# A graph layer with a linear transformer on one core: three PSUM banks for the edge sums, two for VectorE's shared ring

## The reference, cut to what matters

```
xn = layernorm(x)
# 1. graph attention over 100,000 edges, 4 heads of 64
feats = xn @ Ws + bs
score = a_s[src] + a_d[dst] + aw_e * edge_weight + ab
w     = exp(-relu(score / 20))
gnn   = segment_sum(w * feats[dst], src) / segment_sum(w, src)
# 2. four layers of a linear transformer (8 heads of 32, feed-forward of 1024)
for i in range(4):
    h = layernorm(x) * g + b
    q, k = softmax(h @ Wq, over features), softmax(h @ Wk, over nodes)
    x = x + (q @ (k.T @ (h @ Wv))) @ Wo + bo
    x = x + gelu(layernorm(x) * g + b @ W1 + b1) @ W2 + b2
x = x_in + gnn + mix
# 3. slice attention: softmax of 512 slice logits per node, tokens, weighted sums
x = x + slice_attention(layernorm(x))
```

## Time and profile before

| | us |
|---|---|
| median of three runs | 3382.09 (3379.09 to 3383.73) |
| span of the profiled execution | 3482.0 |
| TensorE busy in it | 3221.5 |
| VectorE busy | 2347.5 |
| GpSimd busy | 2056.9 |
| ScalarE busy | 1184.5 |

### The profile page before, as it was taken

The page is one execution under the profiler, slowest core; times in us unless marked ns, Lnnn a source line. Parts: engine busy times, 40 slices in busy tenths (PEclk is TensorE's granted clock), DMA queues, the critical chain, the costliest instruction groups (busy, mean ns, idle before and its releaser), DMA issues.

```text
span 3482.0 us, 43961 instructions
## 1 busy us (share of the span) xinstructions
PE 3221.5 (93%) x13869; PEld 2325.5 (67%) x13869; DVE 2347.5 (67%) x6155; ACT 1184.5 (34%) x2126; POOL 2056.9 (59%) x1776
## 2 busy tenths in 40 slices
PE   8888999999899999999889899898999998999989
PEld 6665667777677777767566666576666666665668
DVE  7998888854454555545677777676666666769951
ACT  3443333333233333323333334243342424422320
POOL 3330577777777777777377677773777777711100
PEclk9999999999999999999999999899999999999999
DMA  3422122222322222322355454454455555422125
GB/s 115 144 96 78 37 50 44 49 49 43 81 47 47 49 50 44 76 55 58 101 136 141 130 138 136 125 141 138 134 152 143 147 147 146 132 82 71 69 101 174
DMA packets 226182, 339.26 MB, mean 97 GB/s; under 512 B 51501, under 2 KB 179755, under 8 KB 225702
## 3 DMA queue, kind: packets, MB, share of 16 engines
q0 software_dynamic: 67840, 119.33, 16.2%
q1 hardware_dynamic: 119502, 162.08, 14.4%
q10 hardware_dynamic: 38616, 55.04, 5.0%
HBM read 248.16 MB, written 87.29 MB: 96 GB/s over the span
## 4 chain that ended last, share of the span: by engine, by line
PE 63%; DVE 21%; issue 5%; another core or an unknown queue 5%; POOL 2%; ACT 2%; DMA 1%; DVEq 1%; ACTq 0%; SPq 0%
PE bank_v L1817 16%; PE bank_a L1804 16%; PE bank_e L1859 8%; PE bank_v L1749 4%; PE bank_a L1721 3%; PE bank_v L1792 3%; PE bank_a L1643 3%; PE bank_v L1709 3%; PE bank_v L1967 2%; POOL arena L804 2%; DVE acc L1503 1%; DVE st L1080 1%; DVEq L1511 1%; DVE arena L1243 1%
## 5 line engine op out<-in xcount | busy, mean ns | idle before, releaser
L804 POOL DMA_INDIRECT arena<-gather_table,arena x880 | 954.7, 1085 | 456.2 <-issue 247.4
L846 POOL DMA_INDIRECT edge_records<-acc x800 | 969.3, 1212 | 402.9 <-issue 402.9
L1817 PE MATMUL bank_v<-W_sb,gT 128*125 128x256 f32 x3200 | 747.1, 385 | 18.3 <-issue 13.7
L1804 PE MATMUL bank_a<-hT,W_sb 128*128 128x500 f32 (+1 forms) x1664 | 716.1, 578 | 13.8 <-issue 12.3
L1817 PEld LDWEIGHTS bank_v<-W_sb,gT 128*125 128x125 f32 x3200 | 602.7, 191 | 122.0 <-issue 26.1
L1804 PEld LDWEIGHTS bank_a<-hT,W_sb 128*128 128x128 f32 x1664 | 317.4, 194 | 326.2 <-issue 307.2
L1859 PE MATMUL bank_e<-arena 128*125 128x260 f32 x1760 | 467.9, 410 | 5.6 <-issue 3.1
L881 ACT ACTIVATE gT<-bank_a,cols 128x500 f32<-128x500 f32 (+1 forms) x416 | 274.2, 661 | 466.1 <-PE bank_a L1804 375.1
L1859 PEld LDWEIGHTS bank_e<-arena 128*125 128x125 f32 x1760 | 327.5, 197 | 57.8 <-issue 7.7
L881 ACT ACTIVATE hT<-bank_a,cols 128x500 f32<-128x500 f32 (+1 forms) x208 | 145.6, 747 | 491.5 <-PE bank_a L1643 378.2
L1239 DVE TENSOR_TENSOR arena<-arena 128x1024 f32<-128x1024 f32 x220 | 268.3, 1220 | 0.0
(11 more groups left out here) (292 smaller groups left out, 4366.1 us busy)
## 6 DMA issues: line engine op xcount, KB each, us to landing
residual<-xs SPq DMA_DIRECT2D x60, 500.0 KB
xs<-residual SPq DMA_DIRECT2D x58, 500.0 KB
arena<-edge_rows ACTq DMA_DIRECT2D x220, 125.0 KB
queries<-qT_out SPq DMA_DIRECT2D x48, 500.0 KB
qT_in<-queries ACTq DMA_DIRECT2D x39, 500.0 KB
arena<-gather_table,arena POOLq DMA_INDIRECT x880
edge_records<-acc POOLq DMA_INDIRECT x800
slice_weights<-arena SPq DMA_DIRECT2D x12, 1000.0 KB, 5.0
```

Of the source, the lines that this page charges most:

```text
L804: e.indirect_dma_start(g_of(j)[:, i, :], None, table_d, bass.IndirectOffsetOnAxis(ap=node[:, TE * j + i:TE * j + i + 1].bitcast(I32), axis ...
L846: e.indirect_dma_start(rec_d, bass.IndirectOffsetOnAxis(ap=pos_i[:, f:f + 1], axis=0), r3[:, f, :], None).then_inc(d_rec, 16)
L1804: o = e.matmul(b[:, 0:n], W[:, k, f * P:(f + 1) * P], hv[:, k, 0:n], start=k == 0, stop=k == KC - 1)
L1817: o = e.matmul(b[0:R, i % 2 * D:(i % 2 + 1) * D], gv[:, f, i * R:(i + 1) * R], W2_sb[:, f * D:(f + 1) * D], start=f == 0, stop=f == FB - 1)
```

## The change

`bank_v` goes from three banks to two and `bank_e` from two to three. The two sums of a block no longer have a bank each: slots 2k and 2k+1 of a rotation over three banks hold the halves of `edge k`, and the score products lie in the bank of slot 2k. TensorE sums the second half of a block in `edge_half k` instead of `edge k`; VectorE adds it there too, and GpSimd's `gather(k+1)` is issued there. The waits follow: TensorE's `edge k` waits for VectorE's second add of `edge_half k-2` instead of the first add of `edge k-1`, and `edge_half k` waits for the first add of `edge k-1`. The list gets two more `edge_half` items.

```diff
-        if k <= NB + 2:
-            blocks.append(((k + 0.5) * apart, ("edge_half", k)))
+        blocks.append(((k + 0.5) * apart, ("edge_half", k)))
...
-        bank_v = [... for i in range(3)]
-        bank_e = [... for i in range(2)]
-        ps_sum = [b[0:R, 0:ROW] for b in bank_e]
-        ps_as = bank_e[0][:, 272:272 + TE * 3 * HG]
+        bank_v = [... for i in range(2)]
+        bank_e = [... for i in range(3)]
+        ps_sum = lambda k, h: bank_e[(2 * k + h) % NE3][0:R, 0:ROW]
+        ps_as = lambda k: bank_e[2 * k % NE3][:, 272:272 + TE * 3 * HG]
...  GpSimd
-                    elif 5 <= k < NB - 1:
-                        e.wait_ge(e_full[1], k - 4)
-                        gather(k + 1)
+                elif stage == "edge_half" and 5 <= at[0] < NB - 1:
+                    k, = at
+                    e.wait_ge(e_full[1], k - 4)
+                    gather(k + 1)
...  VectorE, edge
-                        for h in range(2):
-                            to = accv[:, bass.ds(row_at[h], ROW)]
-                            if h:
-                                e.wait_ge(e_done[0], k - 1)
-                                e.wait_ge(e_full[1], k - 4)
-                            e.tensor_tensor(to, to, ps_sum[h], ALU.add).then_inc(e_done[h], 1)
-                    elif k >= 2:
+                        to = accv[:, bass.ds(row_at[0], ROW)]
+                        e.tensor_tensor(to, to, ps_sum(k, 0), ALU.add).then_inc(e_done[0], 1)
+                    if k >= 2:
                         e.wait_ge(e_done[0], k - 1)
...  VectorE, edge_half, ahead of one_hot_T and one_hot
+                    if k >= 5:
+                        e.wait_ge(e_full[1], k - 4)
+                        to = accv[:, bass.ds(row_at[1], ROW)]
+                        e.tensor_tensor(to, to, ps_sum(k, 1), ALU.add).then_inc(e_done[1], 1)
...  TensorE, edge
-                    if k > 2:
-                        e.wait_ge(e_done[0], k - 2)
+                    if k >= 7:
+                        e.wait_ge(e_done[1], k - 6)
+                    elif k >= 5:
+                        e.wait_ge(e_done[0], k - 4)
...
-                        for h in range(2):
-                            if h and j:
-                                e.wait_ge(e_done[1], j)
-                            for i in range(TH * h, TH * (h + 1)):
+                        for i in range(TH):
...
+                elif stage == "edge_half" and at[0] >= 5:
+                    k, = at
+                    j = k - 5
+                    e.wait_ge(e_done[0], k - 2)
+                    for i in range(TH, TE):
+                        o = e.matmul(ps_sum(k, 1), oh_ring[j % NO][:, i * R:(i + 1) * R], g_of(j)[:, i, :],
+                                     start=i == TH, stop=i == TE - 1)
+                    o.then_inc(e_full[1], 1)
```

More of the change, by code:

```diff
@@ L370, in build_program @@
         bank_a = [ctx.enter_context(nc.psum_tensor(f"bank_a{i}", [P, 512], F32)) for i in range(3)]
-        bank_v = [ctx.enter_context(nc.psum_tensor(f"bank_v{i}", [P, 512], F32)) for i in range(3)]
-        bank_e = [ctx.enter_context(nc.psum_tensor(f"bank_e{i}", [P, 512], F32)) for i in range(2)]
-        ps_sum = [b[0:R, 0:ROW] for b in bank_e]
-        ps_as = bank_e[0][:, 272:272 + TE * 3 * HG]
-        NA, NV = len(bank_a), len(bank_v)
+        bank_v = [ctx.enter_context(nc.psum_tensor(f"bank_v{i}", [P, 512], F32)) for i in range(2)]
+        bank_e = [ctx.enter_context(nc.psum_tensor(f"bank_e{i}", [P, 512], F32)) for i in range(3)]
+        NA, NV, NE3 = len(bank_a), len(bank_v), len(bank_e)
+        ps_sum = lambda k, h: bank_e[(2 * k + h) % NE3][0:R, 0:ROW]
+        ps_as = lambda k: bank_e[2 * k % NE3][:, 272:272 + TE * 3 * HG]
         col_ln = lambda kind, l, c: cols[:, kind * NLN + l * KC + c:kind * NLN + l * KC + c + 1]
@@ L1299, in _ @@
             wls_v = wls_tmp.rearrange("p (c n) -> p c n", c=KC)
+            row_at = [None, None]
             for item in order:
@@ L1491, in _ @@
                         o = e.tensor_reduce(sc_of(k).rearrange("p (t h) -> p t h", h=HG),
-                                            ps_as.rearrange("p (t k h) -> p t h k", t=TE, k=3), AX.X, ALU.add)
+                                            ps_as(k).rearrange("p (t k h) -> p t h k", t=TE, k=3), AX.X, ALU.add)
                         if k < 5:
@@ L1510, in _ @@
                     if 4 <= k <= NB + 3:
-                        row_at = [e.value_load(tids[0:1, i:i + 1], min_val=0, max_val=(NT - 1) * ROW)
-                                  for i in (2 * (k - 4), 2 * (k - 4) + 1)]
+                        i = 2 * (k - 4)
+                        row_at[0] = e.value_load(tids[0:1, i:i + 1], min_val=0, max_val=(NT - 1) * ROW)
                 elif stage == "edge_half":
@@ L1517, in _ @@
                         e.wait_ge(rec_set, 1)
+                    if k >= 5:
+                        e.wait_ge(e_full[1], k - 4)
+                        to = accv[:, bass.ds(row_at[1], ROW)]
+                        e.tensor_tensor(to, to, ps_sum(k, 1), ALU.add).then_inc(e_done[1], 1)
                     if k < NB:
                         one_hot_T(k)
-                    if k >= 3:
+                    if 3 <= k <= NB + 2:
                         one_hot(k - 3)
+                    if 4 <= k <= NB + 3:
+                        i = 2 * (k - 4) + 1
+                        row_at[1] = e.value_load(tids[0:1, i:i + 1], min_val=0, max_val=(NT - 1) * ROW)
                 elif stage == "total":
@@ L1847, in _ @@
                         for i in range(TE):
-                            o = e.matmul(ps_as[:, i * 3 * HG:(i + 1) * 3 * HG], ohT_ring[j % NR][:, i * P:(i + 1) * P],
+                            o = e.matmul(ps_as(k)[:, i * 3 * HG:(i + 1) * 3 * HG], ohT_ring[j % NR][:, i * P:(i + 1) * P],
                                          as3[:, bass.ds(col_at[i // TH], 3 * HG)], start=True, stop=True)
@@ L1854, in _ @@
                         e.wait_ge(oh_set, j + 1)
-                        for h in range(2):
-                            if h and j:
-                                e.wait_ge(e_done[1], j)
-                            for i in range(TH * h, TH * (h + 1)):
-                                o = e.matmul(ps_sum[h], oh_ring[j % NO][:, i * R:(i + 1) * R], g_of(j)[:, i, :],
-                                             start=i == TH * h, stop=i == TH * (h + 1) - 1)
-                            o.then_inc(e_full[h], 1)
+                        for i in range(TH):
+                            o = e.matmul(ps_sum(k, 0), oh_ring[j % NO][:, i * R:(i + 1) * R], g_of(j)[:, i, :],
+                                         start=i == 0, stop=i == TH - 1)
+                        o.then_inc(e_full[0], 1)
                     if 1 <= k <= NB:
```

## The result

| kernel | median us | lowest to highest | ratio to before |
|---|---|---|---|
| before | 3380.64 (4 runs) | 3379.09 to 3383.73 | |
| after | 3451.22 (4 runs) | 3443.47 to 3452.76 | 1.0196, 95% interval 1.018 to 1.0212 |

What follows compares the result with a forecast made beforehand. TensorE was taken as the bound, busy 3221.5 of 3482.0 us, with VectorE almost wholly full in the loop over groups. The terms -45 - 7 + 23 + 19 + 19 + 3 = +12 us gave 3394 us, range 3355 to 3425.

Steps and rivals of the forecast that it cites:

- Part 3(a): Slice logits loop: with two banks TensorE's third tile waits for the first's drain, 2.1 us lost per group, +23 us.
- Part 3(b): 330 to 1700 us: `attend`, `down` and `context` fills wait for VectorE's drains with two banks, +19 us.
- Part 1: Edge stretch: TensorE's waits for VectorE's adds shrink as it may run further ahead, -45 us, bounds -84 and -15.
- Part 2: Clock in the edge stretch: fewer dips behind removed waits, -7 us, bounds -29 and +10.
- Part 3(c): Edge stretch: five fills would start before their bank of two is drained, +19 us, bounds +5 and +30.
- Part 4: Edge stretch: moved work, with gathers released half a block (3 us) later, sums split and VectorE's second add moved, +3 us.
- The lead wins: Rival: edge waits and the clock dips behind them vanish, -31 us, 3351 us; chance 0.23.
- It cancels: Rival: TensorE's small pauses swallow much of the new `bank_v` waits, time within 7 us of 3382; chance 0.20.
- GpSimd becomes the bound: Rival: gathers released 3 us later reach VectorE late in the `up` stretches, +38 us, 3432 us; chance 0.10.

Runs made afterwards that it cites:

- e7: Changed kernel with a free edge bank as third bank of VectorE's shared ring before and after the edge stretch: 3376.72 us, 0.9986 of before.
- e4: The changed kernel unchanged, timed again on chip B: 3442.88 us, 1.018 of before.
- e6: Changed kernel with a free edge bank joining VectorE's shared ring as third from the first slice logits on: 3395.50 us, 1.0037 of before.
- e5: Changed kernel with six useless small matmuls ahead of the third tile of each group's slice logits: 3420.49 us, 1.0117 of before.
- f1: The kernel before, unchanged, profiled again on chip D: 3496.84 us.
- f3: The same kernel as e7, run again on chip D: 3493.24 us, 0.9986 of before.
- e1: Kernel before with two banks in place of three in VectorE's shared ring, nothing else changed, chip A: 3569.48 us, 1.0201 of before.
- e9: The same kernel as e1, run again on chip C: 3570.66 us, 1.0202 of before.
- e2: The change with three banks in the shared ring and two for the edge sums, chip A: 3498.83 us, 1.0002 of before.
- e10: The same kernel as e2, run again on chip C: 3493.42 us, 0.9989 of before.
- f2: Kernel before with each gather in two parts, the first half's rows after the first sums, chip D: 3489.53 us, 0.998 of before.
- e0: The kernel before, unchanged, profiled again on chip A: 3500.78 us.
- e8: The kernel before, unchanged, profiled again on chip C: 3500.66 us.
- f4: The kernel of e7 with each gather in two parts, first half's rows after the first sums, chip D: 3479.04 us, 0.9957 of before.

## Why the prediction was wrong

The direction was right (slower had 0.55); the time was not, and lay outside the range. On chip B, where the parts were switched one by one, the 61.5 us come apart as follows. The edge stretch is what e7 leaves over. Each difference is good to some 5 us.

| step of the prediction | forecast | measured | by |
|---|---|---|---|
| Part 3(a), slice logits loop | +23 | +47.4 | e4 - e6 |
| of it, the wait | +23 | +25.0 | e5 - e6 |
| of it, the clock | not in it | +22.4 | e4 - e5 |
| Part 3(b), 330 to 1700 us | +19 | +18.8 | e6 - e7 |
| Parts 1, 2, 3(c), 4, the edge stretch | -30 | -4.7 | e7 - before |
| sum | +12 | +61.5 | |

**The failed steps.** There are two, of equal size: the price of Part 3(a) was 24 us too low, and the edge stretch, where the -52 us of Parts 1 and 2 were to outweigh the +22 of 3(c) and 4, gave 25 us less than forecast.

**Part 3(a):** "2.1 us lost in all. Nothing covers it" was right as a wait and too small as a price. Behind a wait of 2.14 us in each group the granted clock falls to 0.50 within the first matmul set and stays there for the second, and these sets are on VectorE's path; that costs 2.6 us a group on top. The clock stood in Part 2 with "Waits of part 3 make new ones", inside -7 with +10 as its upper bound, and was never priced for eleven equal waits in a row in the one loop where nothing has slack. The earlier trace rows held the evidence: 0.53 behind a wait of 4.13 us. I took it as a rule for long waits. The row to multiply was at hand: two sets of 1.98 us at half clock are up to 4 us more a group, which is the bound (a) lacked. With e5 the forecast of 21.3 us a group is met exactly, so the mechanism of (a) is shown and its size is what failed.

**Part 3(b)** was right to within the error of the measurement, from starts and drains compared fill by fill: +18.8 us, and the first edge product 20.7 us earlier in e7 than in after. Its sign came as well: outside the loop the profile of after has 37.3 us of waits ahead of `attend`, `down` and `context` fills that a VectorE drain ends (lines 1796, 1821, 1753), where some 40 were forecast and before has 1.7. Of them 16.5 lie in 330 to 1700 us and 17.2 beside the edges.

**Parts 1, 2 and 3(c)** give nearly nothing together. The waits did go, as Part 1 said, and by more (82.8 to 14.5 between profiles of one kind). That the stretch would be shorter by them was the error: f1 against f3 shows 68 us gone at the one line and 55 of them back at others. Part 3(c) did not cost its +19 either, as far as the slower chips show: with the ring of two alone the stretch takes 1354.6 and 1363.3 us (e1, e9), against 1344.0 to 1360.9 in before. So its waits fell into time that was lost anyway, as its lower bound had it. If that holds on chip B as well, Part 1 had nothing to make up for, and of its -45 only a few us came. How the -4.7 splits further was not measured. The lower bound of -15 for Part 1 named pauses in which the other engines stand as well, and two of the rows read had shown them (the "remote" entries of the earlier trace rows). But chip B has no such pauses and gives as little. There another reason is likelier: GpSimd gathers almost without a stop in after and e7, and 868 gathers at 1.086 and 0.3 us take some 1200 of the stretch's 1251 us, an estimate from the rows of after. A stretch so filled can't become much shorter by TensorE's waits. No run here made the gathers fewer or faster on such a chip, so this is argued and not shown.

**Part 4**: splitting costs nothing (e2 1.0002, e10 0.9989). That later gathers cost something is not shown: releasing each half early gives 10 to 14 us back with three edge banks and 7 to 8 in the kernel before (f2). One of its readings was wrong: the "176 us of its idle time waits on TensorE" are 89.5 for TensorE and 86.8 under "remote" in the earlier trace rows. And in Part 2 ten dips of 1.7 to 3.4 us are 17 to 34 us, not up to 29; neither changes the sum.

**The rivals.** *The lead wins* needed under 30 us of new `bank_v` waits; there were 37 outside the loop alone. *It cancels* had (a) at 15 and fell to (a)'s row. *GpSimd becomes the bound* was to decide when the waits at line 1255 passed 40 us. They passed 200, and the 38 us that it priced did not come: with 211 us of them e7 runs at 0.9986. The marker was wrong, since VectorE idles 305 of the 1246.7 us of e7's edge stretch anyway. But what the rival starts from, that gathers fill GpSimd's time, is what the traces of after and e7 show; that the change brought it about they do not.

**The two sections.** By the rule of the Trainium skill, "Perfetto Trace Analysis", section "Optimizing Tensor Performance", that independent groups rotate through banks so that draining overlaps the next matmuls, two banks would have done as far as its words go, for it gives no number; this case's loop went from 19.2 to between 23.0 and 24.6 us with two (e1). The Trainium skill, "Perfetto Trace Analysis", section "Optimization Strategy", says that a gap coming back on the engine that should be full can mean too little PSUM; e6 agrees, where a third bank took the loop back to 19.2 us.

**Open.** There is no profile of before without the pauses, so it isn't known whether the 204 to 216 us of gather waits on such chips are the change's, nor how long before waits for its adds there, nor whether GpSimd is as full in it. On the slower chips before waits 0.5 to 6.5 us for gathers in the whole run (e0, e8, f1), the split with two edge banks 16.3 and 32.7 (e2, e10) and f3 23.3. What the pauses are, the trace does not tell.

## What to carry to other kernels

A new wait on TensorE is priced with the clock behind it: count the matmuls that follow each occurrence and ask what they cost at half clock, above all in a loop where the same wait comes every round. Ask of a shared ring of banks what its shortest stage needs and lend banks by stage rather than for the whole program: the ring was worth 66 us in the stages that did not use the edge banks, and with its gathers in halves the version that lends them (f4) beats both kernels, on the slower chips, where it was timed. And a wait that a change removes is not time gained until the idle time of the whole stretch falls; before pricing it, look for another engine that is as full there, as GpSimd is here.

## What the runs showed of the hardware

- TensorE stood still for 2.14 us up to 3200.82, the granted clock still at 1.00; in the 5.5 us from 3203 on it was 0.50. Such a wait comes once in each group of 23 to 25 us, and the loop runs at 0.88 on the whole. Filling 1.6 us of each with matmuls whose result nobody reads, which left a wait of 0.69, kept the clock at 1.00 and made the kernel 22.4 us faster.
- The same kernel takes 3381 us on one chip and 3497 to 3500 on three others (each chip was used at one time only, so the chip and the time can't be told apart). Of the kernel that is e7 and f3 both kinds were profiled: span 3374.6 us at a mean granted clock of 0.981, and 3492.7 at 0.968. Of the 118 us between them, 17 lie ahead of the first score product (1703.1 and 1720.1), 101 between the first and the last (1246.7 and 1347.3 us), and less than 1 behind. On the slower chips the trace has waits of VectorE, ScalarE and GpSimd put down to "remote", of which two rows of before:

```profile
DVE esc L1491 <- remote: 120.4, 41, 8.0
...
POOL arena L804 <- remote: 86.8, 46, 3.0
```
